# A norm in six chunks, one scan, scores ahead of a product, and a norm's sum on GpSimd, in a block of attention and experts on one core

## What is computed

```python
xn = layernorm(x)
qkv = xn @ w_qkv                                  # q, k, v: 16 heads of 8
scores = causal(q @ k.T / sqrt(8))
attn_out = softmax(scores) @ v
y = attn_out @ w_proj + b_proj + xn
attn = layernorm(y) * gamma + beta
probs = softmax(xn @ Wr.T)                        # 8 experts, the top two kept, not renormalised
ffn = sum over the two: probs[e] * (gelu(xn @ W1[e] + b1[e]) @ W2[e] + b2[e])
out = x + attn + ffn
```

## Time and profile before

| | us |
|---|---|
| median of 3 runs | 848.52 (847.52 to 849.83) |
| the profiled execution, own time | 851.77 |
| its span, first to last instruction | 850.0 |
| prologue with the expert choice, to the first wholly regular step | 0 to 138 |
| regular steps of the attention | 138 to 404 |
| steps with pieces of the expert weights | 404 to 545 |
| last steps and the first expert tile | 545 to 576 |
| expert tiles and last sums | 576 to 850 |

### The profile page before, as it was taken

One profiled execution on the slowest core, in us unless ns is written; L12 is line 12 of the kernel. 1 busy time (PEld: TensorE's weight loads), 2 busy tenths in 40 slices (PEclk: granted clock), 3 DMA queues, 4 the chain that ended last, 5 costly groups with the idle time before them and its releaser, 6 DMA issues.

```text
span 850.0 us, 24989 instructions
## 1 busy us (share of the span) xinstructions
PE 699.9 (82%) x7877; PEld 518.1 (61%) x7878; DVE 692.9 (82%) x1617; ACT 525.4 (62%) x1039; POOL 536.0 (63%) x575
## 2 busy tenths in 40 slices
PE   1366579999999999999888888868999999999800
PEld 1243346666666666666655555537888889888800
DVE  5778878898999998989889999557788888888744
ACT  4541346565656565656556565537989999999800
POOL 8750456767676776767777777334767676667710
PEclk9999899999999999999999999978999999999955
DMA  8294122232323232232233432202222222222189
...
DMA packets 113313, 93.66 MB, mean 110 GB/s; under 512 B 16618, under 2 KB 97650, under 8 KB 113268
## 3 DMA queue, kind: packets, MB, share of 16 engines
...
## 4 chain that ended last, share of the span: by engine, by line
PE 56%; DVE 13%; issue 7%; POOL 7%; DMA 6%; ACT 5%; SPq 5%; DVEq 0%; ACTq 0%; POOLq 0%
PE wide L1259 10%; PE bank_head L1148 7%; PE wide L1113 5%; PE bank_head L1250 5%; PE bank_maxB L1250 5%; PE bank_maxA L1127 4%; PE bank_maxB L1127 3%; DMA xn_rows<-parts_dram 3%; DMA k_cat<-qk_rows 3%; DVE shift L911 3%; POOL probs L581 3%; PE bank_misc L1173 3%; SPq L478 2%; PE bank_maxB L1131 2%; PE bank_maxA L1131 2%
## 5 line engine op out<-in xcount | busy, mean ns | idle before, releaser
L581 POOL TENSOR_SCALAR_AFFINE_SELECT probs<-probs 128x512 f32<-128x512 f32 (+1 forms) x192 | 158.3, 833 | 103.6 <-ACT probs L653 102.8
L653 ACT ACTIVATE probs<-wide 128x1024 f32<-128x1024 f32 x192 | 188.8, 1018 | 47.3 <-PE wide L1117 24.5
L619 POOL DMA_INDIRECT parts_dram<-o_T,dest x144 | 161.0, 1118 | 74.7 <-issue 48.6
L572 POOL DMA_INDIRECT x_slots<-xn_rows,slot_i x128 | 127.3, 995 | 62.8 <-DVE slot_i L868 31.4
L911 DVE TENSOR_REDUCE shift<-bank_maxA 128x2 f32<-128x512 f32 (+1 forms) x192 | 132.1, 688 | 20.1 <-PE bank_maxA L1131 12.9
L911 DVE TENSOR_REDUCE shift<-bank_maxB 128x2 f32<-128x512 f32 (+1 forms) x192 | 131.5, 685 | 4.9 <-PE bank_maxB L1131 0.8
L687 ACT ACTIVATE probs<-wide,b_all 128x256 f32<-128x256 f32 x288 | 121.4, 478 | 16.8 <-PE wide L1259 10.0
L1148 PE MATMUL bank_head<-probs,v_aug 128*32 128x256 f32 (+1 forms) x2048 | 98.9, 334 | 19.1 <-POOL probs L581 18.9
L1259 PE MATMUL wide<-xgT_raw,xnT 128*128 128x256 f16 x864 | 109.2, 277 | 3.7 <-DVE xgT_raw L1020 3.6
L1003 DVE TENSOR_TENSOR probs<-probs 128x512 f16<-128x512 f32 x144 | 99.7, 692 | 5.5 <-ACT probs L693 1.1
L1127 PE MATMUL bank_maxA<-k_cat,q_diag 128*128 128x128 f16 (+1 forms) x512 | 76.2, 252 | 28.5 <-DVE shift L911 19.5
...
## 6 DMA issues: line engine op xcount, KB each, us to landing
qk_rows<-split SPq DMA_DIRECT2D x32, 512.0 KB, 3.2
...
q_diag<-qk_rows SPq DMA_DIRECT2D x256, 32.0 KB
...
x_all<-in_x SPq DMA_DIRECT2D x8, 512.0 KB, 7.6
pieces_f<-in_w SPq DMA_DIRECT2D x8, 512.0 KB, 4.8
```

What stands on the lines that cost most here:

```text
L572: pool.indirect_dma_start(out=x_slots, out_offset=bass.IndirectOffsetOnAxis(ap=slot_i[:, t, c:c + 1], axis=0), in_=xn_rows[:, t, :], in_of ...
L581: pool.affine_select(out=part, in_=part, compare_op=ALU.is_ge, fill=0.0, base=0, pattern=[[0, n], [1, P]], channel_multiplier=-1).then_inc ...
L619: pool.indirect_dma_start(out=parts_dram, out_offset=bass.IndirectOffsetOnAxis(ap=dest[:, of, t:t + 1].bitcast(U32), axis=0), in_=y[:, of ...
L653: act.activation(probs[:, u, :], ps[:, :], ACT.Exp, scale=SCALE).then_inc(empty, 1)
```

## The change

- The norm's moments are taken in six chunks. ScalarE normalises 13 groups, VectorE three. The clear of q_diag on GpSimd is cut in two, the weights are loaded in another order with semaphores of their own, and VectorE's prologue is put in another order.
- The beta adds: four stand behind the expert choice on GpSimd, the other four at m0 of steps 5, 7, 9 and 11.
- The counts of an expert lie side by side; eight scans become one over all experts, with zeros in `goes_on` where an expert begins. The two weights of a token are made at the end of step 2 (`weights`), and sending begins a step later (`SEND = FINISH`), both tiles of a step at m0 (three in every other step from 24 on).
- s5 stands ahead of o0. The projection's stage becomes LAST, its place behind m1 of the next step, and `add_and_measure` goes with it.
- SP issues both halves of q and k in the step that projects them, the second when s5 is filled, ahead of the shifts. Eight transfers of the clear go ahead of the first store.
- VectorE makes only the first product of the norm; ScalarE scales it at the step's end, and GpSimd adds it to x behind s0's mask of the next step. The root moves behind s0's mask too.
- A piece of the expert weights is converted on ScalarE behind v of the step that loads it.

```diff
-        SEND = SOFT
+        SEND = FINISH
...
-            ("maxA", "m0", MAXIMA), ("maxB", "m1", MAXIMA), ("misc", "qk", PROJECT),
+            ("maxA", "m0", MAXIMA), ("maxB", "m1", MAXIMA), ("head", "proj", LAST),
+            ("misc", "qk", PROJECT),
             ("head", "o1", FINISH), ("maxA", "m2", MAXIMA), ("maxB", "m3", MAXIMA),
             ("misc", "v", MAXIMA), ("maxA", "m4", MAXIMA), ("wide0", "s0", SOFT),
             ("maxB", "m5", MAXIMA), ("wide1", "s1", SOFT), ("misc", "oT0", FINISH),
             ("maxA", "m6", MAXIMA), ("maxB", "m7", MAXIMA), ("wide0", "s2", SOFT),
             ("misc", "oT1", FINISH), ("maxA", "m8", MAXIMA), ("maxB", "m9", MAXIMA),
             ("head", "onT", FINISH), ("wide1", "s3", SOFT), ("maxA", "m10", MAXIMA),
-            ("wide0", "s4", SOFT), ("maxB", "m11", MAXIMA), ("head", "o0", SOFT),
-            ("misc", "shift", MAXIMA), ("wide1", "s5", SOFT), ("head", "proj", FINISH),
+            ("wide0", "s4", SOFT), ("maxB", "m11", MAXIMA), ("wide1", "s5", SOFT),
+            ("head", "o0", SOFT), ("misc", "shift", MAXIMA),
...
-        LAST_AFTER, SUM_AFTER, SEND_AFTER = "shift", "s0", ("m0", "s2")
+        LAST_AFTER, SUM_AFTER, SEND_AFTER = "shift", "s0", ("m0", "m0")
...
-                places = ("m0", "s1", "s3") if (s - TAIL) % 2 == 0 else SEND_AFTER
+                places = ("m0", "m0", "m0") if (s - TAIL) % 2 == 0 else SEND_AFTER
...
-        MOMENTS = [(0, 8), (8, 16), (16, 32), (32, 48), (48, 64)]
-        assert NT == 64 and 4 * ACT_GROUPS == MOMENTS[-1][0]
+        ROUTE_DONE = 27
+        ROUTE_WEIGHTS = 31
+        MOMENTS = [(0, 8), (8, 16), (16, 24), (24, 40), (40, 56), (56, 64)]
...
+            def fill_slots(begin, end):
...
-                for c in range(16):
+                for c in range(begin, end):
...
+            def load_experts():
...
                         load_piece(i)
-                if has(s, MAXIMA):
-                    b = s - MAXIMA
-                    if has(s - 1, SOFT):
-                        name, before = use(s - 1, "s5")
-                        sp.wait_ge(filled[name], before + 1)
-                    sp.wait_ge(rows_stored, b * 16 + 16)
-                    sp.nop(nofuse=True)
-                    load_half(b, 1 - par, 1)
-                if isinstance(s, int) and s == MAXIMA:
-                    fill_slots()
                 if has(s, PROJECT):
...
                     load_half(s, par, 0)
+                    if has(s, SOFT):
+                        name, before = use(s, "s5")
+                        sp.wait_ge(filled[name], before + 1)
+                        sp.nop(nofuse=True)
+                    load_half(s, par, 1)
...
+            fill_slots(0, 8)
+            sp.wait_ge(consts, 26)
             step(0, 0)
-            sp.wait_ge(consts, 28)
+            fill_slots(8, 16)
+            load_experts()
...
-            pool.memset(q_diag[:, 0, :, :, :], 0.0).then_inc(consts, 1)
             for c, (begin, end) in enumerate(MOMENTS):
+                if c < 2:
+                    pool.memset(q_diag[:, 0, 2 * c:2 * c + 2, :, :], 0.0).then_inc(consts, 1)
...
-            for c in range(BETA_PARTS):
+            pool.memset(goes_on[:, :, :], 1.0).then_inc(consts, 1)
+            pool.wait_ge(consts, 30)
+            pool.memset(goes_on[:, :, 0], 0.0).then_inc(consts, 1)
+            def add_beta(c):
...
-                wait_normed(pool, 2 * c + 1)
...
-                                   beta_bc[:, :].rearrange("p (o d) -> p o d", o=1).to_broadcast([P, NT // BETA_PARTS, D]), ALU.add).then_inc(offset_ready, 1)
+                                   beta_bc[:, :].rearrange("p (o d) -> p o d", o=1).to_broadcast([P, NT // BETA_PARTS, D]),
+                                   ALU.add).then_inc(res_ready if c == BETA_PARTS // 2 - 1 else offset_ready, 1)
+            wait_normed(pool, ACT_GROUPS - 1)
+            wait_normed(pool, GROUPS - 1)
+            pool.wait_ge(weights_loaded, 64)
+            pool.wait_ge(route, ROUTE_PICKED + 1)
+            for c in range(BETA_PARTS // 2):
+                add_beta(c)
...
+            def add_normed(b):
+                pool.wait_ge(y2_scaled, b * QT + QT)
+                mine = x_all[:, b * QT:(b + 1) * QT, :]
+                pool.tensor_tensor(mine, mine, y2[:, :, :], ALU.add).then_inc(res_ready, 1)
+            def powers(s):
+                b = s - LAST
+                pool.wait_ge(mv2_ready, b * 3 + 3)
+                pool.tensor_tensor(rstd2[:, :], mv2[:, :, 1], half[:, 0:QT], ALU.pow).then_inc(rstd2_ready, 1)
...
-                    pool.wait_ge(route, ROUTE_DONE)
+                    pool.wait_ge(route, ROUTE_WEIGHTS)
...
                         mask(s, int(what[1:]))
...
                         send_tile(t)
+                    if what == "m0" and s in (5, 7, 9, 11):
+                        add_beta(BETA_PARTS // 2 + (s - 5) // 2)
+                    if what == SUM_AFTER and has(s - 1, LAST):
+                        add_normed(s - 1 - LAST)
+                    if what == SUM_AFTER and has(s, LAST):
+                        powers(s)
                     if what == SUM_AFTER and has(s, FINISH):
...
-                if has(s, FINISH):
-                    b = s - FINISH
-                    pool.wait_ge(mv2_ready, b * 3 + 3)
-                    pool.tensor_tensor(rstd2[:, :], mv2[:, :, 1], half[:, 0:QT], ALU.pow).then_inc(rstd2_ready, 1)
+                if s == B + LAST - 1:
+                    add_normed(s - LAST)
...
+                        for i in pieces(s):
+                            high_piece(i)
...
-                for i in pieces(s):
-                    act.wait_ge(piece_loaded[i % 2], 16 * (i // 2 + 1))
-                    act.activation(part_of(i, 0), piece[i % 2], ACT.Copy).then_inc(piece_high, 1)
+                if has(s, LAST):
+                    b = s - LAST
+                    act.wait_ge(rstd2_ready, b * 1 + 1)
+                    act.wait_ge(y2_ready, b * QT + (QT + 1))
+                    for t in range(QT):
+                        act.activation(y2[:, t, :], y2[:, t, :], ACT.Copy, scale=rstd2[:, t:t + 1]).then_inc(y2_scaled, 1)
...
-                then(V.tensor_scalar(xn_rows[:, :, D + 4], best[:, 0, :], -1.0, float(E), ALU.mult, ALU.add))
...
-                then(V.tensor_reduce(padded[:, :], total.rearrange("p (t e) -> p e t", e=E), axis=AX.X, op=ALU.add))
+                then(V.tensor_reduce(padded[:, :], total.rearrange("p (e t) -> p e t", e=E), axis=AX.X, op=ALU.add))
...
-                for e in range(E):
-                    V.tensor_tensor_scan(place[:, :, e], ones[:, :], total.rearrange("p (t e) -> p t e", e=E)[:, :, e],
-                                         padded[:, e:e + 1], ALU.mult, ALU.add).then_inc(route, 1)
-                    route_count += 1
-                dve.wait_ge(exp_router, 2)
-                then(V.tensor_reduce(red[:, :], prob[:, :, :], axis=AX.X, op=ALU.add))
-                then(V.tensor_tensor(rank[:, :, :], wide[1][:, 0:512].rearrange("p (t e) -> p t e", e=E), place[:, :, :], ALU.add))
+                first_tile_total = total.rearrange("p (e t) -> p e t", e=E)[:, :, 0]
+                then(V.tensor_tensor(first_tile_total, first_tile_total, padded[:, :], ALU.add))
+                dve.wait_ge(consts, 31)
+                then(V.tensor_tensor_scan(place_by_expert[:, :, :].rearrange("p e t -> p (e t)"), goes_on[:, :, :].rearrange("p e t -> p (e t)"), total, 0.0,
+                                          ALU.mult, ALU.add))
+                then(V.tensor_tensor(rank[:, :, :], wide[1][:, 0:512].rearrange("p (t e) -> p t e", e=E),
+                                     place_by_expert[:, :, :].rearrange("p e t -> p t e"), ALU.add))
...
-                then(V.reciprocal(xn_rows[:, :, D], red[:, :]))
-                then(V.tensor_tensor(red[:, :], top[:, 1, :], xn_rows[:, :, D], ALU.mult))
-                then(V.tensor_tensor(xn_rows[:, :, D + 2], red[:, :], xn_rows[:, :, D], ALU.subtract))
...
+                    dve.wait_ge(route, route_count - 1)
...
+            def weights():
+                nonlocal route_count
+                dve.wait_ge(exp_router, 2)
+                then(V.tensor_reduce(red[:, :], prob[:, :, :], axis=AX.X, op=ALU.add))
+                V.tensor_scalar(xn_rows[:, :, D + 4], best[:, 0, :], -1.0, float(E), ALU.mult, ALU.add).then_inc(route, 1)
+                route_count += 1
+                then(V.reciprocal(xn_rows[:, :, D], red[:, :]))
+                then(V.scalar_tensor_tensor(out=xn_rows[:, :, D + 2], in0=top[:, 1, :], scalar=-1.0, in1=xn_rows[:, :, D],
+                                            op0=ALU.add, op1=ALU.mult))
+                assert route_count == ROUTE_WEIGHTS, route_count
...
-                b = s - FINISH
+                b = s - LAST
...
+                dve.wait_ge(y2_ready, b * QT + 1)
...
+                dve.wait_ge(res_ready, b * 1 + 1)
...
```

(51 more changed lines are left out.)

46 lines of the change are left out of this document (32 added, 14 removed).

## The result

| | us |
|---|---|
| changed kernel, median of 4 runs | 837.04 (834.98 to 839.47) |
| kernel before, median of 4 runs | 849.17 (847.52 to 851.39) |
| ratio, 95% interval | 0.9857 (0.9818 to 0.9895) |
| profiled execution of the changed kernel, own time | 838.32 |
| its span | 836.6 |

The forecast was 834 with a range of 817 to 847, and 837.8 for the profiled execution. The total came out nearly as said, and that is in good part luck: the prologue was right in cause, most other terms were not, and their errors cancel. That is what most of the following is about. To set the terms against the trace I took the start of a few instructions of TensorE in both traces: `qk` of a step (the projection of q and k), the transpose of the last shift, and the first product of the second expert tile.

A forecast was written before the change was run, and what follows sets the result against it. TensorE was taken to bound the regular steps, with waits in the tail and VectorE stalled beside GpSimd in the prologue. Terms summed to -14.0 from 851.77, 837.8; less 3.25 for the median, 834.5, stated as 834 (range 817 to 847).

The forecast's parts named there:

- Prologue: Ahead of the expert choice: beta adds leave, GpSimd's clear is halved, first chunk starts sooner; 13.0 us less (9 to 16).
- The term for the adds: Prologue: VectorE's scaling and subtract-and-multiply operations are slow beside GpSimd's beta adds; removing these excesses saves 10.4 us.
- Places: Expert choice: eight scans become one and short operations leave the chain; 2.0 us less (0.8 to 2.9).
- the strided count: Expert choice: the counting product reads its picks with a stride; cost between nothing and 0.66 us.
- A usual step: Regular attention steps: projection moved behind the next step's m1 saves 0.33 us a step, x19 = -6.3 us (0 to -11).
- The gain at m6: Second half of k loaded earlier: no gain counted in a usual step, only -0.7 us in step 3.
- The term for GpSimd: Usual step: more sends and three operations for one, yet masks end level with o0; 0, with 0 to +0.5 a step.
- GpSimd the bound: Rival, attention steps: o0 waits 0.45 us for GpSimd in each of 27 steps, 846 us; chance 0.13.
- The late adds in steps 5 to 11: Steps 5, 7, 9, 11: a beta add behind the sends makes GpSimd late by 1.2 us each; +5 us (0 to +9).
- SP's queue: Loads issued ahead of the shifts: shifts begin later but about 0.4 us slack is left; cost 0.
- The tail: Nine steps with expert pieces: k waits removed, ScalarE's wait for a piece added; +2 us (-8 to +10).
- The end: Projection's last pass adds a step, ScalarE waits for the norm, the last piece is ready sooner; 0 (-2 to +3).

The follow-up runs named there:

- e1: Changed kernel with all eight beta adds back in GpSimd's prologue, none behind the picks or in steps 5 to 11; 849.57 us.
- e10: e9 with the picks stored expert by expert, so both counting products read in order and VectorE writes and reads them with a stride; 822.28 us.
- e4: Changed kernel with VectorE's split of a piece at the end of the step that converts it, not ahead of the next step's add; 834.93 us.
- e6: Changed kernel with ScalarE's conversion of a piece at the end of its step in place of behind v; 829.96 us.
- e5: Changed kernel with the projection and its add back at the end of the step that makes its input, behind shift; 847.90 us.
- e3: Changed kernel with o1 behind m3 in place of behind qk, on every engine; 830.18 us.
- e8: Changed kernel with s5 back behind o0 and shift, the projection staying behind m1 of the next step; 878.15 us.
- e9: e7 with the four beta adds behind the picks replaced: one half there, the other fifteen one a step in steps 5 to 19; 817.85 us.
- e2: Changed kernel with the second half of q and k loaded where it was before, a step later, behind a piece; 852.82 us.
- e7: Changed kernel with the edits of e3 and e6, and the four late beta adds cut in eight halves, one a step in steps 5 to 12; 819.92 us.

## Why the prediction was right, and where it was not

**Prologue (13.0 forecast, 15.07 measured).** Right in cause: e1 shows 12.42 us for the adds, the chunks and the order keep 2.65. The term for the adds (10.4) was a little low. What the 13.0 leaves for the rest, 2.6, agrees with that, but it was taken from near the middle of 9 and 16 and not worked out, so the fit is luck in part; no run takes the chunks or the order back alone.

**Places (2.0 forecast).** The scan and the operations that left the chain came out as said or better, and the weights at the end of step 2 cost TensorE no wait. The mis-sized term is the strided count, which I bounded by 0 and 0.66: it costs 1.37 (e10). A second one I had left out: the sum of ranks reads the places with a stride and takes 1.02 in place of 0.69. From the first operation (line 883) to the last slot the places take 9.9 us in place of 10.67, 0.8 less. The Trainium skill, SBUF — State Buffer, section "SBUF: two separate sides", had spoken against this edit, and its rule was the better guide; the bound from a plain sum of 512 was taken from the wrong engine.

**First loop step.** Between qk 4 and qk 5 the changed kernel shows 19.45 us (19.38 before); e4 and e6, whose code is the same there, show 17.01 and 18.43, the other runs 16.77 to 18.77 and one, e5, 20.83. The granted clock tells part of it (stretch 107 to 112 us of after, then of e4, then a stretch of before behind the same work; the third figure from the end is the clock):

```profile
107.00:112.00 5.00, 4.69 (x45) 2.93 (x46) 2.91 (x10) 0.60 (x1) 0.45 (x1) 0.50 0.32 119
```

```profile
107.00:112.00 5.00, 4.99 (x65) 3.64 (x58) 4.54 (x12) 2.81 (x4) 0.67 (x2) 1.00 0.33 122
```

```profile
125.00:130.00 5.00, 4.82 (x27) 2.88 (x28) 3.88 (x8) 1.52 (x3) 0.04 (x1) 0.66 0.28 105
```

In this execution of the changed kernel TensorE waited 3.57 us ahead of o1, while VectorE packs the experts, and then ran at 0.50, the level of 1.2 GHz; in e4 it waited 3.58 in the same place and ran on at 1.00. The kernel before fell too, behind a wait of 3.89. So the 0.63 that stands against 1.7 compares two executions in which the clock fell; without a fall the changed kernel's code takes up to 2.4 us less here (e4), and what the kernel before would take then is open.

**A usual step (6.3 forecast, -0.6 with the late adds).** The step that failed is "I take 0.33 a step, the middle". (The middle of nothing and 0.60 is 0.30, 5.7 us over the steps; that changes little.) Of the 0.60 that I called the price of the projection, 0.45 is its own work and only 0.15 a wait; and o1's wait for the add could have been worked out from rows that were there: two maxima and an add behind m0, 0.6 + 0.6 + 0.4 us, against m1, the projection and qk on TensorE. I named this wait and priced it by halving. The gain at m6, which I had as 0 in a usual step, was 0.12 on average. e3 shows that 0.4 a step was there to be had, with o1 behind m3. The term for GpSimd, 0, was right, and its rival (GpSimd the bound) did not come: in the step shown the masks of s0 to s2 end at 259.41, and o0 starts at 260.02. One reading for it was off: GpSimd's add replaced only half of VectorE's two products, as ScalarE's scaling (0.68) took the other half, so that pair could not show what an add costs on either engine.

**The late adds in steps 5 to 11 (5 forecast, 0 measured).** With 112.53 us for eight steps against 112.68 without them, the term fails as a price of the changed kernel; the mechanism (GpSimd late by the add less its idle time) shows in e3 with 3.3 us, where o1's wait is gone. The slack ahead of s0's mask, which I had at about 1.1, is 1.67 in the changed kernel.

**SP's queue (0 forecast).** Right: s0 doesn't wait for the shifts in a regular step. That it is an edge is shown by e8, where this wait appears with 0.70.

**The tail (-2 forecast, 1.0 gained).** The waits for k (4.9 us) went, as said. ScalarE's wait was 0.6 to 0.8 in four steps and 1.9 and 2.3 in two, in place of 2.7: I took the landing from one row, 6.1 us, where the median over the pieces of before is 4.8 and that of after 4.0. I also left out that o0 and o1 waited 8.5 us for GpSimd's masks there, of which 1.8 are left. What I overlooked on the other side is the split: I followed ScalarE's conversion and not VectorE's operation, which stands at "proj" and moved with it. It makes o1 wait 1.42, in place of 0.37, in seven steps.

**The end (0 forecast, -2.66).** From the last shift to the second tile it takes 35.59 us, before 33.94, in e1, e3, e4, e6 and e9 33.06 to 33.83, in e2, e7 and e10 34.4 to 35.0, in e5 and e8 36.8 to 37.2. So up to 2 us of it may be this execution; whether the added last step costs the rest is open, and was not tried.

Errors in both directions cancelled: the prologue 2 us better, the steps up to the regular ones 1 worse, the regular ones 2 worse, the tail 3 better, the end 2.7 worse.
